# Turning H of groups 3 to 15 by a transposing DMA instead of by TensorE in a hypergraph layer

## The chip, the cores and the metric

The kernel runs on one core of one Trainium2 chip. The metric is the device time of one execution in microseconds (us); lower is better. Each instruction stream (TensorE, VectorE, ScalarE, GpSimd and SyncE, in the profile PE, DVE, ACT, POOL and SP) works through its own queue in order and waits on semaphores that the others raise. PEld is TensorE's weight load, which runs beside its matmuls. SP does no arithmetic here; it only issues DMAs.

## The reference

64 graphs of 128 nodes with 256 features each. `adj` is a 128x128 matrix of each graph, about one entry in eight of which is not zero.

```python
H   = (adj != 0)                       # [n, c, e]
w   = adj[:, 0, :]                     # first row of adj: the weight of each hyperedge
Dn  = 1 / sum_e H * w                  # 0 where the sum is not positive
Be  = 1 / sum_c H                      # members of each hyperedge; 0 where none
conv(x, W, b) = Dn * (H @ (Be * (H^T @ (x @ W^T)))) + b

h = layer_norm(relu(conv(x, W1, b1))) * gamma + beta       # 512 wide
y = conv(h, W2, b2) + x                                    # 256 wide
out = layernorm(x + y)
```

## The kernel before

**Tiling.** Four graphs make a group (`PER = 4`), sixteen groups the run (`G = 16`). Everything of a group lies as 128 partitions x 4 graphs x columns. The two convolutions of a graph share one matrix, A = Dn H Be H^T, which is made once in 128x128 and then applied to x (before W1) and to the second layer's product (after W2).

**How A is made.** VectorE compares `adj_sb` with zero and writes `h_sb` in bf16 (`make_h`, L533). TensorE turns the four 128x128 blocks into the PSUM bank `bank_h` (`turn_h`, L201 to L207). ScalarE copies them to `ht_sb` in f32, block by block, and sums each row on the way, which counts the members of each hyperedge (`read_ht`, L393 to L401: per block one ACTIVATE and one read of the accumulator). VectorE inverts the counts (`make_b`), ScalarE scales (`make_htb`, L408), TensorE multiplies (`make_s`, L217), ScalarE scales by Dn (`make_a`, L416), TensorE turns the result (`turn_a`), and ScalarE stores it as `at_sb` (`read_at`, L424). H is prepared three groups ahead of its use in the second half of a group, and `h_sb`, `ht_sb` have two buffers each.

**The two layers.** `make_u` (L238) is A x; `make_v` (L253) is u W1^T, four chunks k = 0 to 3 of six matmuls each, since u and W1 are split into a high and a low part; `relu` (L436) and `square` (L443) on ScalarE take a chunk each from the two halves of `bank_v` in turn; GpSimd and VectorE split r into `r_hi` (L789) and `r_lo` (L595); `make_g` (L261, L263, L268) is r W2^T, one graph at a time; `read_g` (L586) applies the first normalisation, `make_y` (L285) applies A in two halves of two graphs, `make_z` (L615) adds the residual and `normalise` (L448) finishes.

**What sets the order.** All five streams are written out by hand, one iteration per group, with semaphores between them; there is no scheduler. TensorE's iteration i is: g(i,0), u(i+1), s(i+2), g(i,1), v(i+1,0), g(i,2), turn_q(i), turn_a(i+2), g(i,3), v(i+1,1), turn_h(i+3), v(i+1,2), v(i+1,3), y(i,0), y(i,1). The piece of ScalarE's iteration beside the end of it is relu(i+1,1), read_ht(i+3), relu(i+1,2), square(i+1,1), relu(i+1,3), square(i+1,2), square(i+1,3), make_htb(i+3). `make_y(i, 1)` needs the half of `bank_v` that relu(i+1,3) reads, so it waits for it. SyncE's iteration is the load of adj(i+6), the load of x(i+3), which waits for GpSimd's `add_b2` (L781), and the store of group i-1. Turns of H stand in TensorE's queue for groups 0 to 2 in the preamble and iteration 0, and for groups 3 to 15 in iterations 0 to 12; iteration 13 and later have none.

Of the kernel before, what the change touches and what calls it, by code (L numbers as in the profile page):

```python
# [6 lines left out]
ACT = mybir.ActivationFunctionType  # L7
F32 = mybir.dt.float32
F32R = mybir.dt.float32r
BF16 = mybir.dt.bfloat16  # L10

P = 128
PER = 4
# [6 lines left out]
def hypergraph_block(nc, x, adj, W1, b1, gamma, beta, W2, b2, out):  # L20
# [4 lines left out]
    G = N // PER  # L25
# [8 lines left out]
    with ExitStack() as ctx:  # L34
        def sb(name, shape, dt=F32):
            return ctx.enter_context(nc.sbuf_tensor(name, shape, dt))

        def sem(name):
            return ctx.enter_context(nc.semaphore(name))
# [28 lines left out]
        x_sb = sb("x_sb", [P, 3, PER, DIN])  # L68
        xb_sb = sb("xb_sb", [P, 2, PER, DIN])
        h_sb = sb("h_sb", [P, 2, PER, P], BF16)  # L70
        ht_sb = sb("ht_sb", [P, 2, PER, P])
        members = sb("members", [P, PER])
        binv = sb("binv", [P, 2, PER])
# [31 lines left out]
        bank_h_bf = bank_h.bitcast(BF16)  # L105
        s_parts = bank_s[:, :, 0:2 * HCOLS].rearrange("p b (n e) -> p b n e", n=2)
        last_z = [bank[:, 0:DOUT] for bank in (bank_v[:, 0], bank_v[:, 1], bank_h, bank_q)]
        SUM = DOUT

        weights_in = [sem(f"weights_in{n}") for n in range(4)]  # L110
        edges_in, edges_turned, edges_ready = sem("edges_in"), sem("edges_turned"), sem("edges_ready")
# [8 lines left out]
        w2_hi_ready, w2_ready = sem("w2_hi_ready"), sem("w2_ready")  # L120
        beta_ready, c2_made, c2_ready = sem("beta_ready"), sem("c2_made"), sem("c2_ready")
        h_ready, h_turned, ht_ready = sem("h_ready"), sem("h_turned"), sem("ht_ready")
        b_step, b_ready, htb_ready, wcol_ready = sem("b_step"), sem("b_ready"), sem("htb_ready"), sem("wcol_ready")
        s_made, degree_step, d_ready = sem("s_made"), sem("degree_step"), sem("d_ready")
        a_ready, a_turned, at_ready = sem("a_ready"), sem("a_turned"), sem("at_ready")
# [10 lines left out]
        def graph(n):  # L136
            return slice(n * P, (n + 1) * P)

        def graphs(half):
            return slice(0, PER) if half is None else slice(half * (PER // 2), (half + 1) * (PER // 2))  # L140

        def each(half):
            return range(PER)[graphs(half)]

        def landed(j, ring):

            return 16 * (j // ring + 1)
# [5 lines left out]
        @block.sync  # L153
        def _(sp):
            def load_adj(j):
                if j >= 3:
                    sp.wait_ge(h_ready, j - 2)
                sp.dma_start(adj_sb[:, j % 3], adj_dram[:, j * PER:(j + 1) * PER]).then_inc(adj_in[j % 3], 16)

            def load_x(j):  # L160
                if j >= 3:
                    sp.wait_ge(u_made, (j - 2) * KD)
                    sp.wait_ge(xb_ready, j - 2)
                sp.dma_start(x_sb[:, j % 3], x_dram[:, j * PER:(j + 1) * PER]).then_inc(x_in[j % 3], 16)

            def store(i, half=None):
                part, n = graphs(half), len(each(half))
                if half is None:
                    sp.wait_ge(out_ready, i + 1)
                else:  # L170
                    sp.wait_ge(last_out_ready, half + 1)
                sp.dma_start(out_dram[:, i * PER + part.start:i * PER + part.start + n],
                             z_sb[:, i % 2, part]).then_inc(stored[i % 2], 16)

            load_adj(0)
            sp.dma_start(w1_raw[:, :, :], W1.rearrange("(k p) d -> p k d", p=P)).then_inc(weights_in[1], 16)
            sp.dma_start(w2_raw[:, :, :], W2.rearrange("(k p) h -> p k h", p=P)).then_inc(weights_in[2], 16)
            load_x(0)
            load_adj(1)
            load_adj(2)  # L180
            load_x(1)
            sp.dma_start(b2_half[:, :], b2.unsqueeze(0).to_broadcast([P, DOUT])).then_inc(weights_in[3], 16)
            load_adj(3)
            load_x(2)
            load_adj(4)
            load_adj(5)
            for i in range(G):
                if i + 6 < G:
                    load_adj(i + 6)
                if i + 3 < G:  # L190
                    load_x(i + 3)
                if i >= 1:
                    store(i - 1)
            for half in range(2):
                store(LAST, half)
            sp.wait_ge(stored[0], 16 * (G // 2))
            sp.wait_ge(stored[1], 16 * (G // 2) + 16)

        @block.tensor
        def _(pe):  # L200
            def turn_h(j):  # L201
                pe.wait_ge(h_ready, j + 1)
                if j:
                    pe.wait_ge(at_ready, j)
                for n in range(PER):
                    mm = pe.transpose(bank_h_bf[:, graph(n)], h_sb[:, j % 2, n], ident_b[:, :])
                mm.then_inc(h_turned, 1)  # L207
# [49 lines left out]
            def make_g(i, n):  # L257
                for k in range(KH):
                    if n == 0:
                        pe.wait_ge(r_hi_ready, i * KH + (k + 1))  # L260
                    pe.matmul(bank_g[:, n, 0:W2COLS], r_hi[:, i % 2, k, graph(n)], w2_hi[:, k],  # L261
                              start=(k == 0), stop=False)
                    pe.matmul(bank_g[:, n, 0:DOUT], r_hi[:, i % 2, k, graph(n)], w2_lo[:, k], start=False, stop=False,  # L263
                              skip_group_check=True)
                for k in range(KH):
                    if n == 0:
                        pe.wait_ge(r_lo_ready, i * KH + (k + 1))
                    mm = pe.matmul(bank_g[:, n, 0:W2COLS], r_lo[:, i % 2, k, graph(n)], w2_hi[:, k], start=False,  # L268
                                   stop=(k == KH - 1))
                if n == PER - 1 or (i == LAST and n == PER // 2 - 1):  # L270
                    mm.then_inc(g_made, 1)

            def turn_q(i):
                pe.wait_ge(q_ready, i + 1)
                pe.wait_ge(q_summed, i)
                pe.wait_ge(a_ready, min(i + 3, G))
                for n in range(PER):
                    mm = pe.transpose(bank_q[:, graph(n)], q_sb[:, graph(n)], ident[:, :])
                mm.then_inc(q_turned, 1)
# [61 lines left out]
            for i in range(G):  # L341
                last = i == LAST
                make_g(i, 0)
                if i == 0:
                    turn_h(2)
                if not last:
                    make_u(i + 1)
                if 0 < i and i + 2 < G:
                    make_s(i + 2)
                if i == 0:  # L350
                    pe.wait_ge(c2_ready, 1)
                make_g(i, 1)
                if i == 0:
                    make_s(2)
                if last:
                    turn_q(i)
                else:
                    make_v(i + 1, 0)
                make_g(i, 2)
                if not last:  # L360
                    turn_q(i)
                if i + 2 < G:
                    turn_a(i + 2)
                make_g(i, 3)
                if last:
                    break
                make_v(i + 1, 1)
                if i + 3 < G:
                    turn_h(i + 3)
                make_v(i + 1, 2)  # L370
                make_v(i + 1, 3)
                make_y(i, 0)
                make_y(i, 1)
# [17 lines left out]
        @block.scalar  # L391
        def _(act):
            def read_ht(j):  # L393
                act.wait_ge(h_turned, j + 1)
                act.wait_ge(b_ready, j)
                if j >= 2:
                    act.wait_ge(s_made, j - 1)
                for n in range(PER):
                    ins = nc.scalar.activation(ht_sb[:, j % 2, n], bank_h_bf[:, graph(n)], ACT.Copy,
                                               accum_out=members[:, n:n + 1])  # L400
                ins.then_inc(ht_ready, 1)  # L401

# [125 lines left out]
        def _(dve):  # L528
            def make_h(j):
                dve.wait_ge(adj_in[j % 3], landed(j, 3))  # L530
                if j >= 2:
                    dve.wait_ge(h_turned, j - 1)
                nc.vector.tensor_scalar(h_sb[:, j % 2], adj_sb[:, j % 3], 0.0, None,  # L533
                                        ALU.not_equal).then_inc(h_ready, 1)

# [25 lines left out]
            def make_var1(i, half=None):  # L561
                part, done = graphs(half), i + (half or 0)
                dve.wait_ge(g_made, done + 1)
                nc.vector.tensor_scalar(stat1[:, 0, part], bank_g[:, part, SUM], 1.0 / HID, None,  # L564
                                        ALU.mult).then_inc(stat1_step, 1)
# [189 lines left out]
            for half in range(2):  # L755
                dve.wait_ge(rstd2_ready, G + half)
                for n in each(half):
                    ins = nc.vector.tensor_scalar(z_sb[:, 1, n], last_z[n], mean2[:, 1, n:n + 1],
                                                  rstd2[:, 1, n:n + 1], ALU.add, ALU.mult)
# [112 lines left out]
```

## Time and profile before

| | us |
|---|---|
| median of 3 runs | 301.17 (300.36 to 301.25) |
| the profiled execution | 300.86 |
| its span, first to last instruction | 299.1 |
| TensorE busy | 285.9 (96%) |
| VectorE, ScalarE, GpSimd busy | 207.1, 207.4, 133.7 |
| mean granted TensorE clock | 0.988 of full speed |

The table is read so: TensorE's queue is nearly full, the other three are not, and the whole run has fifteen periods of nearly equal length with a start of some 24 us before them and a tail of some 10 us behind them. Busy time is what the hardware records of instructions; matmuls overlap, so a busy TensorE need not be one that does all it could.

### The profile page before, as it was taken

To read this page: it belongs to the slowest core of one execution; us is meant where nothing else is said; L and a number is where in the kernel's file an instruction comes from. 1 tells how busy PE (TensorE), PEld (TensorE's weight loads), DVE (VectorE), ACT (ScalarE), POOL (GpSimd) and SP (SyncE) were. 2 spreads that over 40 slices of the span, in tenths; PEclk is the share of its full clock that TensorE was granted. 3 is DMA by queue.
4 is the path that set the end of the run, shared out by engine and by line. 5 is a ranking of instruction groups with operands and counts; after the bars stand their busy time and mean duration, and the time that the engine had idled before them with its cause. 6 is when DMAs were issued, how large, how long until landed. Compare 5 with 4: busy or idle time off the path is not lost.

```text
span 299.1 us, 5864 instructions
## 1 busy us (share of the span) xinstructions
PE 285.9 (96%) x1918; PEld 254.5 (85%) x1918; DVE 207.1 (69%) x589; ACT 207.4 (69%) x619; POOL 133.7 (45%) x162
## 2 busy tenths in 40 slices
PE   5799999999999999999999999999999999999972
PEld 5689889798988989898898979898897989988851
DVE  1783686794939587593958669494958759394965
ACT  3498577868687786868677786858778686756430
POOL 2233444617353552636344361735355263636441
PEclk9999999999999999999999999999999999999995
DMA  7921030503114050502305050310304040101112
GB/s 217 297 72 36 1 107 0 175 2 125 56 30 148 0 179 0 172 7 57 120 1 175 2 176 2 109 34 8 133 3 140 2 141 0 59 13 37 37 50 90
DMA packets 26437, 22.55 MB, mean 75 GB/s; under 512 B 860, under 2 KB 26152, under 8 KB 26408
## 3 DMA queue, kind: packets, MB, share of 16 engines
q1 hardware_dynamic: 26304, 22.15, 23.5%
q8 instruction: 15, 0.25, 0.3%
q14 instruction: 14, 0.11, 0.1%
q10 hardware_dynamic: 104, 0.04, 0.0%
HBM read 13.80 MB, written 8.39 MB: 74 GB/s over the span
## 4 chain that ended last, share of the span: by engine, by line
DVE 32%; POOL 27%; issue 23%; PE 11%; ACT 3%; DMA 2%; DVEq 0%; POOLq 0%; SPq 0%
POOL xb_sb L781 11%; DVE r_lo L595 7%; POOL rstd L774 7%; DVE g_sb L586 6%; DVE bn_sb L623 6%; DVE z_sb L615 6%; POOL rstd L796 5%; PE bank_v L253 4%; POOL r_hi L789 4%; DVE mv_sb L633 2%; DMA w_raw<-in_L_gnn_W_dram 2%; PE bank_v L238 1%; POOL shift L801 1%; DVE mean L636 1%; DVE u_lo L558 1%
## 5 line engine op out<-in xcount | busy, mean ns | idle before, releaser
L789 POOL TENSOR_SCALAR r_hi<-r_sb 128x512 fp32r<-128x512 f32 x64 | 48.2, 753 | 82.4 <-ACT r_sb L436 82.4
L261 PE MATMUL bank_g<-w_hi,r_hi 128*128 128x258 f32 x256 | 69.3, 303 | 0.0
L263 PE MATMUL bank_g<-w_lo,r_hi 128*128 128x256 f32 x256 | 63.8, 281 | 0.0
L436 ACT ACTIVATE r_sb<-bank_v,vec 128x512 f32<-128x512 f32 x64 | 44.2, 690 | 15.8 <-PE bank_v L253 15.8
L253 PE MATMUL bank_v<-u_hi,w_hi 128*128 128x512 f32 x128 | 51.9, 406 | 0.4 <-DVE u_lo L558 0.4
L253 PE MATMUL bank_v<-u_lo,w_hi 128*128 128x512 f32 x128 | 50.5, 395 | 0.0
L253 PE MATMUL bank_v<-u_hi,w_lo 128*128 128x512 f32 x128 | 50.4, 394 | 0.0
L263 PEld LDWEIGHTS bank_g<-w_lo,r_hi 128*128 128x128 f32 x256 | 48.4, 189 | 1.0
L261 PEld LDWEIGHTS bank_g<-w_hi,r_hi 128*128 128x128 f32 x256 | 48.3, 189 | 1.1
L595 DVE TENSOR_TENSOR r_lo<-r_sb,r_hi 128x512 fp32r<-128x512 f32 x64 | 47.6, 747 | 1.5 <-POOL r_hi L789 1.5
L268 PE MATMUL bank_g<-w_hi,r_lo 128*128 128x258 f32 x256 | 41.3, 283 | 0.0
L796 POOL TENSOR_TENSOR rstd<-var,half_power 128x4 f32<-128x4 f32 (+1 forms) x17 | 16.7, 980 | 51.3 <-DVE var L637 51.3
L781 POOL TENSOR_TENSOR xb_sb<-x_sb,b_half 128x1024 f32<-128x1024 f32 x16 | 38.2, 2385 | 2.7 <-DVE q_sb L606 2.7
L443 ACT ACTIVATE sq_sb<-r_sb 128x512 f32<-128x512 f32 x64 | 38.3, 625 | 0.5
L586 DVE SCALAR_TENSOR_TENSOR g_sb<-bank_g,rstd,c 128x256 f32<-128x256 f32 x64 | 26.6, 477 | 17.1 <-POOL rstd L774 17.1
L430 ACT ACTIVATE u_hi<-bank_v 128x512 fp32r<-128x512 f32 x32 | 19.0, 598 | 26.5 <-PE bank_v L238 26.5
L564 DVE TENSOR_SCALAR stat<-bank_g 128x4 f32<-128x4 f32 (+1 forms) x17 | 2.7, 161 | 50.1 <-PE bank_g L268 50.1
L448 ACT ACTIVATE z_sb<-z_sb,shift,rstd 128x256 f32<-128x256 f32 x60 | 33.0, 614 | 3.2 <-POOL shift L801 3.2
L268 PEld LDWEIGHTS bank_g<-w_hi,r_lo 128*128 128x128 f32 x256 | 35.2, 189 | 0.0
L285 PE MATMUL bank_v<-g_sb,at_sb 128*128 128x256 f32 x120 | 31.9, 388 | 0.1
L238 PE MATMUL bank_v<-at_sb,x_sb 128*128 128x128 f32 x256 | 31.3, 275 | 0.7 <-ACT at_sb L424 0.7
L238 PEld LDWEIGHTS bank_v<-at_sb,x_sb 128*128 128x128 f32 x256 | 30.0, 192 | 0.9 <-ACT at_sb L424 0.9
(95 smaller groups left out, 485.2 us busy)
## 6 DMA issues: line engine op xcount, KB each, us to landing
x_sb<-in_x_dram SPq DMA_DIRECT2D x16, 512.0 KB, 3.8
out_dram<-z_sb SPq DMA_DIRECT2D x15, 512.0 KB, 4.6
adj_sb<-in_adj_dram SPq DMA_DIRECT2D x16, 256.0 KB, 5.0
w_raw<-in_L_gnn_W_dram SPq DMA_DIRECT2D x2, 512.0 KB, 6.2
out_dram<-z_sb SPq DMA_DIRECT2D x2, 256.0 KB, 2.2
b_half<-in_L_gnn_b_dram SPq DMA_DIRECT2D x1, 128.0 KB, 7.3
edge_rows<-in_adj_dram ACTq DMA_DIRECT2D x1, 32.0 KB, 3.2
vec_rows<-in_L_gnn_b_dram ACTq DMA_DIRECT2D x1, 2.0 KB
```

The source lines that it names most:

```text
L238: mm = pe.matmul(bank_v[:, c, graph(n)], x_sb[:, j % 3, n, graph(c)], at_sb[:, j % 3, n], start=True, stop=True)
L253: mm = pe.matmul(bank_v[:, k % 2], w[:, c, graph(k)], u[:, c], start=(m == 0), stop=(m == len(terms) - 1))
L261: pe.matmul(bank_g[:, n, 0:W2COLS], r_hi[:, i % 2, k, graph(n)], w2_hi[:, k], start=(k == 0), stop=False)
L263: pe.matmul(bank_g[:, n, 0:DOUT], r_hi[:, i % 2, k, graph(n)], w2_lo[:, k], start=False, stop=False, skip_group_check=True)
L268: mm = pe.matmul(bank_g[:, n, 0:W2COLS], r_lo[:, i % 2, k, graph(n)], w2_hi[:, k], start=False, stop=(k == KH - 1))
L436: nc.scalar.activation(r_sb[:, k], bank_v[:, k % 2], ACT.Relu, bias=vec[:, k:k + 1]).then_inc(relu_ready, 1)
L443: nc.scalar.activation(sq_sb[:, k], r_sb[:, k], ACT.Square).then_inc(sq_ready, 1)
L448: ins = nc.scalar.activation(z_sb[:, i % 2, n], z_sb[:, i % 2, n], ACT.Identity, bias=shift2[:, n:n + 1], scale=rstd2[:, 0, n:n + 1])
L586: ins = nc.vector.scalar_tensor_tensor(out=g_sb[:, n], in0=bank_g[:, n, 0:DOUT], scalar=rstd1[:, n:n + 1], in1=c2[:, :], op0=ALU.mult, op1 ...
L595: nc.vector.tensor_tensor(r_lo[:, i % 2, k], r_sb[:, k], r_hi[:, i % 2, k].bitcast(F32), ALU.subtract).then_inc(r_lo_ready, 1)
L781: nc.gpsimd.tensor_tensor(xb_sb[:, i % 2], x_sb[:, i % 3], b2_half[:, :].unsqueeze(1).to_broadcast([P, PER, DOUT]), ALU.add).then_inc(xb_r ...
L789: nc.gpsimd.tensor_scalar(r_hi[:, i % 2, k], r_sb[:, k], 1.0, 1.0, ALU.mult, ALU.mult).then_inc(r_hi_ready, 1)
```

## The change

H of groups 3 to 15 goes through a new buffer in SBUF, `turned_h`, which has the shape and the type of `h_sb` and two buffers. SyncE issues one transposing DMA per group, which reads the four blocks of `h_sb` and writes their transposes side by side. It waits for the comparison of its group, for the transposing DMA before it, and, from group 5 on, for ScalarE's reading of the buffer that it overwrites. `read_ht` takes its blocks from `turned_h` instead of PSUM, and `make_h` waits for the DMA where it waited for TensorE's turn. TensorE keeps the turns of groups 0 to 2.

```diff
@@ sync @@
+            def turn_h(j):
+                sp.wait_ge(h_ready, j + 1)
+                if j > ON_PE:
+                    sp.wait_ge(h_dma_turned, 16 * (j - ON_PE))
+                if j >= ON_PE + 2:
+                    sp.wait_ge(ht_ready, j - 1)
+                sp.dma_start_transpose(turned_h[:, j % 2], h_sb[:, j % 2].rearrange("p n c -> p (n c)")).then_inc(
+                    h_dma_turned, 16)
...
             load_adj(5)
+            turn_h(3)
             for i in range(G):
                 if i + 6 < G:
                     load_adj(i + 6)
+                if i + 4 < G:
+                    turn_h(i + 4)
                 if i + 3 < G:
                     load_x(i + 3)
@@ tensor @@
                 make_v(i + 1, 1)
-                if i + 3 < G:
-                    turn_h(i + 3)
                 make_v(i + 1, 2)
@@ scalar, read_ht @@
-                act.wait_ge(h_turned, j + 1)
+                if j < ON_PE:
+                    act.wait_ge(h_turned, j + 1)
+                else:
+                    act.wait_ge(h_dma_turned, 16 * (j - ON_PE + 1))
...
-                    ins = nc.scalar.activation(ht_sb[:, j % 2, n], bank_h_bf[:, graph(n)], ACT.Copy,
+                    source = bank_h_bf[:, graph(n)] if j < ON_PE else turned_h[:, j % 2, n]
+                    ins = nc.scalar.activation(ht_sb[:, j % 2, n], source, ACT.Copy,
@@ vector, make_h @@
-                if j >= 2:
+                if 2 <= j < ON_PE + 2:
                     dve.wait_ge(h_turned, j - 1)
+                elif j >= ON_PE + 2:
+                    dve.wait_ge(h_dma_turned, 16 * (j - 2 - ON_PE + 1))
```

TensorE's queue in iteration 0, where v(1,1) ends and v(1,2) begins (`bank_v` is written from the split u and W1; L253 before is L268 of the changed kernel). Before:

```order
109 L253 MATMUL bank_v<-u_hi,w_hi 128x512
110 L253 MATMUL bank_v<-u_hi,w_lo 128x512
111 L253 MATMUL bank_v<-u_lo,w_hi 128x512
112 L206 MATMUL bank_s<-ident_b,h_sb 128x128 [waits at_ready,h_ready]
113 L206 MATMUL bank_s<-ident_b,h_sb 128x128 x3
114 L253 MATMUL bank_v<-u_hi,w_hi 128x512 [waits relu_ready]
115 L253 MATMUL bank_v<-u_hi,w_lo 128x512
```

and in the changed kernel:

```order
109 L268 MATMUL bank_v<-u_hi,w_hi 128x512
110 L268 MATMUL bank_v<-u_hi,w_lo 128x512
111 L268 MATMUL bank_v<-u_lo,w_hi 128x512
112 L268 MATMUL bank_v<-u_hi,w_hi 128x512 [waits relu_ready]
113 L268 MATMUL bank_v<-u_hi,w_lo 128x512
```

The four turning matmuls are gone and the next chunk of v follows at once; the other rows keep their order. SyncE's queue in iterations 1 and 2, one load of adj, one of x and one store each. Before:

```order
12 L158 DMA adj_sb<-in_adj_dram 128x4x128 [waits h_ready]
13 L164 DMA x_sb<-in_x_dram 128x4x256 [waits xb_ready,u_made]
14 L172 DMA out_dram<-z_sb 128x4x256 [waits out_ready]
15 L158 DMA adj_sb<-in_adj_dram 128x4x128 [waits h_ready]
16 L164 DMA x_sb<-in_x_dram 128x4x256 [waits xb_ready,u_made]
17 L172 DMA out_dram<-z_sb 128x4x256 [waits out_ready]
```

and in the changed kernel:

```order
15 L161 DMA adj_sb<-in_adj_dram 128x4x128 [waits h_ready]
16 L175 DMA_TRANSPOSE turned_h<-h_sb 128x4x128 [waits ht_ready,h_dma_turned,h_ready]
17 L167 DMA x_sb<-in_x_dram 128x4x256 [waits xb_ready,u_made]
18 L184 DMA out_dram<-z_sb 128x4x256 [waits out_ready]
19 L161 DMA adj_sb<-in_adj_dram 128x4x128 [waits h_ready]
20 L175 DMA_TRANSPOSE turned_h<-h_sb 128x4x128 [waits ht_ready,h_dma_turned,h_ready]
21 L167 DMA x_sb<-in_x_dram 128x4x256 [waits xb_ready,u_made]
22 L184 DMA out_dram<-z_sb 128x4x256 [waits out_ready]
```

The transposing DMA stands between the load of adj and the load of x, so both that load and the store behind it are queued behind its three waits.

## Rows read from the trace of the kernel before

**Rows 1.** The page: busy time, share of the span and instructions of each engine
```profile
PE 285.9 (96%) x1918; PEld 254.5 (85%) x1918; DVE 207.1 (69%) x589; ACT 207.4 (69%) x619; POOL 133.7 (45%) x162
```

**Rows 2.** Timeline of PE: start us, duration us, engine, line, operation, out<-in, count
```profile
139.76 0.39 PE L253 MATMUL bank_v<-u_lo,w_hi 128*128 128x512 f32 x1
139.99 0.40 PE L206 MATMUL bank_s<-ident_b,h_sb 128*128 128x128 bf16 x4
140.19 0.48 PE L253 MATMUL bank_v<-u_hi,w_hi 128*128 128x512 f32 x1
140.51 0.39 PE L253 MATMUL bank_v<-u_hi,w_lo 128*128 128x512 f32 x1
```

**Rows 3.** Timeline of PE: the y matmuls of iterations 11, 12 and 13
```profile
228.77 2.13 PE L285 MATMUL bank_v<-g_sb,at_sb 128*128 128x256 f32 x8
...
245.91 2.13 PE L285 MATMUL bank_v<-g_sb,at_sb 128*128 128x256 f32 x8
...
262.77 0.38 PE L285 MATMUL bank_v<-g_sb,at_sb 128*128 128x256 f32 x1
```

**Rows 4.** Timeline of PE: y of one iteration, its fourth and fifth record alone
```profile
143.08 2.13 PE L285 MATMUL bank_v<-g_sb,at_sb 128*128 128x256 f32 x8
143.72 0.38 PE L285 MATMUL bank_v<-g_sb,at_sb 128*128 128x256 f32 x1
144.11 0.45 PE L285 MATMUL bank_v<-g_sb,at_sb 128*128 128x256 f32 x1
```

**Rows 5.** Timeline of ACT beside it; in brackets idle time before, and its releaser
```profile
140.18 0.69 ACT L436 ACTIVATE r_sb<-bank_v,vec 128x512 f32<-128x512 f32 x1 [0.66 <-PE bank_v L253]
140.77 0.27 ACT L399 ACTIVATE ht_sb<-bank_s 128x128 f32<-128x128 bf16 x1
...
141.02 0.28 ACT L399 ACTIVATE ht_sb<-bank_s 128x128 f32<-128x128 bf16 x1
...
141.87 0.69 ACT L436 ACTIVATE r_sb<-bank_v,vec 128x512 f32<-128x512 f32 x1
142.46 0.62 ACT L443 ACTIVATE sq_sb<-r_sb 128x512 f32<-128x512 f32 x1
143.28 0.69 ACT L436 ACTIVATE r_sb<-bank_v,vec 128x512 f32<-128x512 f32 x1 [0.19 <-PE bank_v L253]
143.86 1.14 ACT L443 ACTIVATE sq_sb<-r_sb 128x512 f32<-128x512 f32 x2
```

**Rows 6.** Groups of ACT, 100 to 240 us: busy us, mean ns of one, idle before
```profile
L408 ACT ACTIVATE htb_sb<-ht_sb,binv 128x128 f32<-128x128 f32 x32 | 10.2, 393 | 0.0
L416 ACT ACTIVATE a_sb<-bank_s,dinv 128x128 f32<-128x128 f32 x33 | 9.5, 368 | 9.9 <-DVE dinv L545 9.9
```

**Rows 7.** Timelines of DVE and of PEld behind read_g of the same iteration
```profile
141.22 1.66 DVE L586 SCALAR_TENSOR_TENSOR g_sb<-bank_g,rstd,c 128x256 f32<-128x256 f32 x4 [0.99 <-POOL rstd L774]
...
145.20 0.69 DVE L595 TENSOR_TENSOR r_lo<-r_sb,r_hi 128x512 fp32r<-128x512 f32 x1
...
146.25 0.19 PEld L268 LDWEIGHTS bank_g<-w_hi,r_lo 128*128 128x128 f32 x1
```

**Rows 8.** Timelines of DVE (the comparison) and of SP's DMA issues
```profile
139.55 0.38 SPq L172 DMA_DIRECT2D out_dram<-z_sb  x1
...
152.12 0.42 DVE L533 TENSOR_SCALAR h_sb<-adj_sb 128x512 bf16<-128x512 f32 x1
...
156.13 0.37 SPq L164 DMA_DIRECT2D x_sb<-in_x_dram  x1
```

**Rows 9.** Timelines of DVE and ACT at the start: comparison and reading of group 3
```profile
25.11 0.42 DVE L533 TENSOR_SCALAR h_sb<-adj_sb 128x512 bf16<-128x512 f32 x1
...
37.91 0.27 ACT L399 ACTIVATE ht_sb<-bank_s 128x128 f32<-128x128 bf16 x1
```

**Rows 10.** The page: a DMA queue (packets, MB, share of 16 engines) and issues (KB, us to landing)
```profile
q1 hardware_dynamic: 26304, 22.15, 23.5%
...
out_dram<-z_sb SPq DMA_DIRECT2D x15, 512.0 KB, 4.6
```

More of the change, by code:

```diff
@@ L70, in hypergraph_block @@
         h_sb = sb("h_sb", [P, 2, PER, P], BF16)
+        turned_h = sb("turned_h", [P, 2, PER, P], BF16)
         ht_sb = sb("ht_sb", [P, 2, PER, P])
@@ L108, in hypergraph_block @@
         SUM = DOUT
+        ON_PE = 3
         weights_in = [sem(f"weights_in{n}") for n in range(4)]
@@ L122, in hypergraph_block @@
         h_ready, h_turned, ht_ready = sem("h_ready"), sem("h_turned"), sem("ht_ready")
+        h_dma_turned = sem("h_dma_turned")
         b_step, b_ready, htb_ready, wcol_ready = sem("b_step"), sem("b_ready"), sem("htb_ready"), sem("wcol_ready")
```

## The prediction

> **What bounds the kernel now.** The page's busy line comes first: TensorE is busy for 96% of the span and no other engine for more than 69% [rows 1]. The next view is TensorE's timeline, to see whether "busy" is a queue that never waits. From one y to the next the iterations repeat at 245.91 - 228.77 = 17.14 us [rows 3], and inside one the matmuls follow at a fixed step; only at y does one come late. The first four records of y step by (143.72 - 143.08) / 3 = 0.21 us, so the fifth was due at 143.93 and starts at 144.11, 0.18 us late [rows 4]. It begins the second half of y, which waits for ScalarE's fourth relu: that starts at 143.28, lasts 0.69 and ends at 143.97 [rows 5]. So a period is TensorE's own work with one short stall, and a change is worth what it takes out of TensorE's queue, as long as the chains on ScalarE and VectorE beside it can move up by as much. That is the question here; the profiled execution took 300.86 us, 0.31 below the median of 301.17, and the sum is made on the first and carried over to the second.
>
> **What is removed from TensorE.** In an iteration the four turning matmuls start at 139.99, 0.23 after the last matmul of v(i+1,1) at 139.76, which is that chunk's own step. The first two matmuls of v(i+1,2) start at 140.19 and 140.51 [rows 2]. Without the turns these two would start at 139.99 and 140.22, so the four cost 140.51 - 140.22 = 0.29 us; the start at 140.19 shows nothing, because the next step behind it is 0.32 instead of 0.23. The trace holds a control for this number: iteration 13 has no turn. Its y starts at 262.77, 16.86 us after that of iteration 12, against 17.14 before [rows 3]. The difference is 0.28 us, and in iteration 13 TensorE did take it. There are 13 such iterations (0 to 12), which makes 13 x 0.28 = 3.6 us if nothing else holds.
>
> The Trainium skill, "VectorE: DVE Perf Modes", section "The three transpose paths", gives 390 ns for a 128x128 bf16 transpose on TensorE, which for four would be an estimated 1.56 us per group and 20 us in all. The trace disagrees: four in a row take 0.28 us out of the queue.
>
> **What iteration 13 does not test: ScalarE.** It has no read_ht either, and the change keeps read_ht, with another source. The chain is relu(k=1) at 140.18, read_ht from 140.77, relu(k=2) at 141.87, square at 142.46, relu(k=3) at 143.28 [rows 5]. The blocks of read_ht step by 141.02 - 140.77 = 0.25, so four of them leave ScalarE free at 141.77; relu(k=2) waited 0.10 more for TensorE. Reading SBUF instead of PSUM costs more: no row shows this copy from SBUF in bf16, but the two scaled 128x128 copies differ by their source, 393 ns from SBUF and 368 from PSUM [rows 6], 0.025 more. The lower bound is then nothing (a two-byte source may be no dearer), the upper one twice the row's difference, 0.05 per block, since the step can grow by more than the duration; the row's value, 0.03, is taken. With 4 x 0.03 = 0.12 relu(k=2) starts at 141.89, square at 142.48. A relu behind a square can start 0.52 after it (two squares last 1.14 together and one alone 0.62 [rows 5]), so at 143.00. TensorE's v(i+1,3) would be done for a start at 143.28 - 0.28 = 143.00. The fourth relu moves up by the whole 0.28; by the upper bound, relu(k=3) starts at 143.08 and moves up by 0.20. The 0.18 stall of y stays, since both sides move together.
>
> **VectorE behind it.** Its queue from read_g at 141.22 is anchored to the end of g(i,3), which lies ahead of the removed turns, and runs without a gap to r_lo(k=3), at 145.20 for 0.69, done 145.89. TensorE loads that as a weight in g(i+1,0) at 146.25 [rows 7], and 0.28 earlier at 145.97. The margin falls from 0.36 to 0.08. What a handover costs is bounded by nothing below and, from the nearest row, by the 0.14 between the end of the relu at 143.97 and the y matmul at 144.11 [rows 4, 5]; with that one the weight is ready at 146.03, and 0.06 of the gain is lost. Between 0.22 and 0.28 I take 0.26, because on both chains the middle value still fits. Each shorter period ends at the next g(i+1,3), from which VectorE's queue starts anew, so the loss does not add up. The sum: 13 x 0.26 = 3.4 us; 300.86 - 3.4 = 297.5 for an execution like the profiled one, 301.17 - 3.4 = **297.8** as median. The ends are 13 x 0.20 = 2.6 and 13 x 0.29 = 3.8.
>
> **What is added: 13 transposing DMAs.** No row shows one. In steady state the comparison that feeds it ends at 152.12 + 0.42 = 152.54 [rows 8]. By ScalarE's row this H is read one iteration later than its turn would now be possible: read_ht of the iteration shown is at 140.77 [rows 5], that of the next at 157.9, and the H made at 152.12 belongs to the one after that, at 140.77 + 34.3 = 175.1. The cover is 22.5 us. For group 3, at the start, it is from 25.53 to 37.91, 12.4 us [rows 9]. The price from below is the nearest ordinary transfer, a store of 512 KB that lands 4.6 us after its issue [rows 10]; this one has 128 KB. The price from above follows from pieces: the queue's 26,304 packets took 23.5% of 16 engines' time over the span of 299.1 us, 42.8 ns each [rows 10]; 65,536 pieces of one element each would take 65,536 x 42.8 ns / 16 = 175 us. I take about 5 us, since rows of 256 bytes and more, 512 pieces, come to 1.4 us by the same rate and the landing dominates. Then all of it is covered.
>
> The Trainium skill speaks against the change here: "VectorE: DVE Perf Modes", section "Rules for kernel authors", advises TensorE for a 128x128 transpose whenever PSUM will do as destination, and the table of "The three transpose paths" gives 1309 ns per block on the DMA path. Four would be an estimated 5.2 us, inside the cover, so the sum would be the same by it.
>
> **What it moves on queues.** SyncE's queue gains one issue per iteration, and its wait ends at 152.54, while the load of x behind it goes at 156.13 anyway for another reason [rows 8]. If SyncE is held for less than 3.6 us per transpose, neither the load nor the store behind it moves at all; an ordinary issue holds it for 0.37 to 0.38. If it is held longer, the store (139.55 + 17.15 = 156.70 in that period) slides, and what it must beat is VectorE's writing of the same z buffer a group later, just ahead of r_lo(k=3) two periods on from 145.20, so about 178.9. With 4.6 to land there are over 17 us left. VectorE's comparison waits for a transpose of two groups earlier, done 20 us before. ScalarE's `read_ht` gets the only new wait that matters: behind it are relu(k=2), the squares and relu(k=3), and TensorE's v, y and g wait for those.
>
> **Rivals.**
> 1. *The gain is taken up by ScalarE or VectorE.* If a read from `turned_h` steps by 0.055 to 0.08 more (the fourth relu moves up by 0.40 less four times that), or GpSimd and VectorE slow each other in the new alignment, a period shrinks by 0.07 to 0.18: 1 to 2.3 us, 298.9 to 300.3. For it: three chains are within 0.1 us of each other. Against: iteration 13 took the full 0.28 with two of them in place.
> 2. *Nothing is gained, since the read grows by 0.10 per block.* relu(k=2) then starts at 142.17, 0.30 later than now, relu(k=3) at 143.28 again, and the time is 301 within 0.9. For it: no row of this form. Against: the SBUF reads of rows 6 are 0.025 apart from the PSUM ones.
> 3. *Slower: the transposing DMA is the new bound.* If the DMA works in pieces so small that it takes longer than a period, the loop runs at the DMA's time T, because each transpose waits for the one before, ScalarE waits in read_ht, and everything waits for ScalarE: 301.2 + 13 x (T - 17.15). It decides from T = 17.15 us, which is 6,400 pieces of 42.8 ns on 16 engines, or 20 bytes a piece; at T = 20 the time is 338, and at one piece per element (175 us) 2,350. For it: a transpose in two-byte elements has no long rows on both sides. Against: nothing in the trace. The same sign comes at a small size if T is between 12.4 and 17: only the first turn is late, by under 5 us, once, which the gain nearly repays.
> 4. *The change does not do what it says*, in that TensorE stays as long although its turns are gone. Iteration 13 excludes it but for rival 2.
>
> **How the numbers follow.** My forecast, the whole or nearly the whole of 0.20 to 0.29 per iteration, has 0.62: 13 x that gives 297.4 to 298.6, with the spread of the runs (0.4) 297.0 to 299.0. Rival 1 has 0.13, rivals 2 and 4 together 0.11, rival 3 and other slowdowns by over 0.9 us 0.10; 0.04 is left for below 297.0. The measurement can tell about 0.3%, 0.9 us, from no change. So faster is 0.62 + 0.13 + 0.04 = 0.79, within 0.3% 0.11, slower 0.10. For eight in ten the range takes the forecast, rival 1 and the near part of rival 2: 296.9 to 300.7.
>
> **What would show it.** Right: the y matmuls 16.86 to 16.9 us apart in iterations 1 to 12 and unchanged in 13; no turning matmul beyond the first three groups; ScalarE's blocks of read_ht 0.25 to 0.30 apart with no idle time before the first; the load of x still released by GpSimd. Wrong by rival 1: a later fourth relu or a weight load of r_lo that waits. Wrong by rival 3: ScalarE idle before read_ht with a DMA as releaser, SyncE waiting for transposes, and the store late. The forecast fails if the transposing DMA holds SyncE or the DMA engines for a large part of a period, or if its traffic slows engines that read SBUF, for which no row gives a price.

## The result, and the profile after

The changed kernel takes 299.65 us (median of 20 runs, 299.42 to 301.02) against 301.12 (median of 20 runs of the kernel before beside it). The ratio is 0.9965, 95% interval 0.9954 to 0.9976: faster, by about 1.05 us. (The medians lie 1.47 us apart. Executions of either kernel scatter over more than 1 us; the means of the 20 differ by 1.07, and the ratio follows these.) One execution of e8_split_g_wait took 1,585 us and is left out of its ratio. The forecast was faster by 3.4 us, to 297.8. The sign was right and the time lies in the range, but the gain is under a third of the one forecast.

The page of the changed kernel, its busy line, its DMA queue and the issues of the new kind (no KB are given for it; the last number is the median us from issue to landing):

```profile
PE 284.8 (96%) x1866; PEld 253.0 (85%) x1866; DVE 209.9 (70%) x589; ACT 206.8 (69%) x619; POOL 132.9 (45%) x162
...
q1 hardware_dynamic: 33376, 23.86, 27.1%
...
turned_h<-h_sb SPq DMA_TRANSPOSE x13, 2.4
```

TensorE has lost its 52 turning matmuls (x1918 to x1866, [rows 1]) but its busy time fell by only 1.1 us, and VectorE, of which nothing was removed or added, is busy for 2.8 us more. The transposing DMAs land after 2.4 us, at most 3.6, far inside the cover of 12 and 22 us.

The timeline of TensorE gives the period by its y matmuls, as [rows 3] do for the kernel before:

```profile
39.76 2.17 PE L300 MATMUL bank_v<-g_sb,at_sb 128*128 128x256 f32 x8
...
56.84 2.17 PE L300 MATMUL bank_v<-g_sb,at_sb 128*128 128x256 f32 x8
...
261.91 2.13 PE L300 MATMUL bank_v<-g_sb,at_sb 128*128 128x256 f32 x8
...
277.42 2.13 PE L300 MATMUL bank_v<-g_sb,at_sb 128*128 128x256 f32 x8
```

A period is 17.08 to 17.10 us, where 16.86 to 16.9 was forecast and 17.14 was before. The y of iteration 14, the last of this form, stands at 277.42 against 278.28 before, 0.86 us earlier. The first y brings 0.46 of that (39.76 against 40.22). It has the removed turn of iteration 0 ahead of it, worth 0.28; the rest belongs to the start, which varies from one execution to the next: in e1_dma_beside below, with the same queue on TensorE as before, the first y stands at 41.12. The twelve intervals up to iteration 12 bring 0.63, 0.05 each instead of 0.28. And the interval to iteration 13, which was 16.86 before, is 17.09 now and gives 0.23 back. The profiled executions themselves differ by more, 300.86 and 299.62; the other 0.4 us lies in the tail. From the y at 278.28 to the end of the span there are 20.8 us before and 20.3 after, and the granted clock of the last slice was 0.5 before and 0.8 after. The change isn't the reason: e1_dma_beside and e5_order_on_before keep every turn on TensorE, and from their y of iteration 14 to the end there are 20.3 and 20.5 us.

So something new ends late in each period. First VectorE's queue and GpSimd in the kernel before, two instructions of each (r_lo and r_hi are one line for every chunk; r_lo(k) and r_hi(k) are those of chunk k, in order):

```profile
142.79 1.01 DVE L595 TENSOR_TENSOR r_lo<-r_sb,r_hi 128x512 fp32r<-128x512 f32 x1
...
144.01 0.68 DVE L595 TENSOR_TENSOR r_lo<-r_sb,r_hi 128x512 fp32r<-128x512 f32 x1
...
142.64 0.62 POOL L789 TENSOR_SCALAR r_hi<-r_sb 128x512 fp32r<-128x512 f32 x1 [0.94 <-ACT r_sb L436]
144.04 1.12 POOL L789 TENSOR_SCALAR r_hi<-r_sb 128x512 fp32r<-128x512 f32 x1 [0.78 <-ACT r_sb L436]
```

VectorE's queue behind read_g in the changed kernel, the place of [rows 7]:

```profile
140.77 1.66 DVE L605 SCALAR_TENSOR_TENSOR g_sb<-bank_g,rstd,c 128x256 f32<-128x256 f32 x4 [0.99 <-POOL rstd L793]
142.35 1.01 DVE L614 TENSOR_TENSOR r_lo<-r_sb,r_hi 128x512 fp32r<-128x512 f32 x1
...
143.57 0.89 DVE L614 TENSOR_TENSOR r_lo<-r_sb,r_hi 128x512 fp32r<-128x512 f32 x1
144.38 0.68 DVE L634 SCALAR_TENSOR_TENSOR z_sb<-xb_sb,bank_v 128x512 f32<-128x512 f32 x1
144.98 0.68 DVE L614 TENSOR_TENSOR r_lo<-r_sb,r_hi 128x512 fp32r<-128x512 f32 x1
```

GpSimd beside it, r_hi of k = 2 and 3 and the small copy behind them:

```profile
142.20 0.62 POOL L808 TENSOR_SCALAR r_hi<-r_sb 128x512 fp32r<-128x512 f32 x1 [0.94 <-ACT r_sb L453]
143.29 0.62 POOL L808 TENSOR_SCALAR r_hi<-r_sb 128x512 fp32r<-128x512 f32 x1 [0.47 <-ACT r_sb L453]
143.87 0.64 POOL L787 COPY htb_sb<-edge_cols 128x4 f32<-128x4 f32 x1
```

And TensorE's matmuls and its weight loads at the end of g(i+1,0) and the start of u:

```profile
142.29 2.17 PE L300 MATMUL bank_v<-g_sb,at_sb 128*128 128x256 f32 x8
145.26 0.83 PE L283 MATMUL bank_g<-w_hi,r_lo 128*128 128x258 f32 x4
145.93 1.95 PE L253 MATMUL bank_v<-at_sb,x_sb 128*128 128x128 f32 x16
...
145.14 0.75 PEld L283 LDWEIGHTS bank_g<-w_hi,r_lo 128*128 128x128 f32 x4
```

r_lo(2) takes 0.89 us. In the kernel before, the same instruction took 0.68 at 144.01, and GpSimd's r_hi(3), 0.03 behind it at 144.04, took 1.12. Now r_hi(3) starts at 143.29, 0.28 ahead of r_lo(2), and takes 0.62: which of the two starts first has changed, because the fourth relu, and with it r_hi(3), moved up with TensorE, while VectorE's queue did not. r_lo(3) is done at 144.98 + 0.68 = 145.66. The four weight loads of r_lo, 0.12 apart, would have the last at 145.50; four in 0.75 us, each 0.19 long, put it at 145.70. TensorE waits 0.19 us there in every period, and the next matmuls (u) start 0.67 after the first of r_lo, where it was 0.49 before.

That closes the account of a period. The turns take 0.29 out of it (from the first matmul of v(i+1,1) to y: 4.48 us before, 4.19 after), the wait for r_lo(3) puts 0.19 back, and ScalarE puts 0.04 back: its fourth relu moved up by 0.25 and not by 0.29 (it stands 2.85 behind the second one, 3.10 before), so the second half of y starts 1.07 behind the first instead of 1.03. What is left is 0.06, and the periods show 0.05.

A second, smaller delay of the same kind lies ahead of it. VectorE's statistics after g(i,3) contain one product of two 128x4 tiles in SBUF:

```profile
155.59 0.21 DVE L586 TENSOR_TENSOR stat<-stat 128x4 f32<-128x4 f32 x1
...
153.40 2.38 POOL L800 TENSOR_TENSOR xb_sb<-x_sb,b_half 128x1024 f32<-128x1024 f32 x1
```

It starts while GpSimd's add (153.40 to 155.78) still runs and takes 0.21; before, the add ended at 138.92, the product started at 139.00 and took 0.16. Together VectorE's chain is about 0.26 us longer than the forecast had it.

The Trainium skill, "SBUF — State Buffer", section "SBUF: two separate sides", says that VectorE and GpSimd share one pair of SBUF ports, and that where VectorE has two inputs in SBUF and GpSimd reads SBUF, the one that starts first keeps the pair for its whole instruction while the other stands still. No trace shows the ports, but the times agree: r_hi(3) ends at 143.91 and r_lo(2) 0.55 behind it, at 144.46, though it started 0.34 before that end; r_lo(1) of the kernel before ends 0.54 behind r_hi(2) (143.80 and 143.26). The other way round, r_hi(3) of the kernel before ends 0.47 behind r_lo(2) (145.16 and 144.69). In these rows the one that starts second ends some half a microsecond behind the end of the first, however long it has waited.

### The profile page after: what moved, and what is told of

Same layout as the page of the kernel before. It is cut to its first block, busy times and chain, and to the rows that moved or that the text cites. A ratio compares the mean times of both kernels' runs of the same rounds, so it can differ in the third digit from the quotient of the medians.

```text
span 297.7 us, 5772 instructions
## 1 busy us (share of the span) xinstructions
PE 284.8 (96%) x1866; PEld 253.0 (85%) x1866; DVE 209.9 (70%) x589; ACT 206.8 (69%) x619; POOL 132.9 (45%) x162
## 3 DMA queue, kind: packets, MB, share of 16 engines
q1 hardware_dynamic: 33376, 23.86, 27.1%
## 4 chain that ended last, share of the span: by engine, by line
DVE 34%; POOL 28%; issue 25%; PE 8%; ACT 3%; DVEq 0%; POOLq 0%
POOL xb_sb L800 11%; DVE r_lo L614 8%; POOL rstd L793 7%; DVE bn_sb L642 7%; DVE z_sb L634 6%; DVE g_sb L605 6%; POOL rstd L815 5%; POOL r_hi L808 4%; PE bank_v L268 3%; DVE mv_sb L652 2%; PE bank_s L333 1%; POOL shift L820 1%; DVE mean L655 1%; DVE u_lo L577 1%; ACT ht_sb L416 1%
## 5 line engine op out<-in xcount | busy, mean ns | idle before, releaser
L808 POOL TENSOR_SCALAR r_hi<-r_sb 128x512 fp32r<-128x512 f32 x64 | 41.8, 654 | 78.0 <-ACT r_sb L453 78.0
L614 DVE TENSOR_TENSOR r_lo<-r_sb,r_hi 128x512 fp32r<-128x512 f32 x64 | 50.3, 790 | 1.5 <-POOL r_hi L808 1.5
L268 PE MATMUL bank_v<-u_hi,w_hi 128*128 128x512 f32 x128 | 50.9, 397 | 0.4 <-DVE u_lo L577 0.4
L268 PE MATMUL bank_v<-u_lo,w_hi 128*128 128x512 f32 x128 | 50.6, 395 | 0.0
L268 PE MATMUL bank_v<-u_hi,w_lo 128*128 128x512 f32 x128 | 50.5, 394 | 0.0
L283 PE MATMUL bank_g<-w_hi,r_lo 128*128 128x258 f32 x256 | 43.8, 288 | 0.0
L283 PEld LDWEIGHTS bank_g<-w_hi,r_lo 128*128 128x128 f32 x256 | 36.1, 189 | 1.7
L253 PE MATMUL bank_v<-at_sb,x_sb 128*128 128x128 f32 x256 | 31.3, 275 | 0.7 <-ACT at_sb L441 0.7
L433 ACT ACTIVATE a_sb<-bank_s,dinv 128x128 f32<-128x128 f32 x60 | 17.2, 369 | 21.0 <-DVE dinv L564 21.0
```

The lines of the kernel that those rows point to most:

```text
L268: mm = pe.matmul(bank_v[:, k % 2], w[:, c, graph(k)], u[:, c], start=(m == 0), stop=(m == len(terms) - 1))
L614: nc.vector.tensor_tensor(r_lo[:, i % 2, k], r_sb[:, k], r_hi[:, i % 2, k].bitcast(F32), ALU.subtract).then_inc(r_lo_ready, 1)
L808: nc.gpsimd.tensor_scalar(r_hi[:, i % 2, k], r_sb[:, k], 1.0, 1.0, ALU.mult, ALU.mult).then_inc(r_hi_ready, 1)
```

## The experiments

The theory: the gain was lost to this collision. The rivals: the transposing DMAs or their hold on SyncE cost it (traffic), or ScalarE's dearer reads from SBUF do. The fences show the main lines of each edit.

### e1_dma_beside: the transposing DMAs alone, beside the old kernel

```diff
             load_adj(5)
+            turn_h(3)
...
                     load_adj(i + 6)
+                if i + 4 < G:
+                    turn_h(i + 4)
```

`make_h` also waits for the transposing DMA of two groups earlier, as in the changed kernel.

> The kernel before, with the 13 transposing DMAs added at the places of the change and nobody reading what they write; TensorE keeps all its turns and ScalarE reads PSUM. Collision theory (the gain was lost because GpSimd's r_hi(3) now runs first and holds up VectorE's r_lo(2)): the DMAs cost nothing, 301.1 us, ratio 1.000 within 0.001, y matmuls 17.14 us apart. Traffic rival (the transposing DMAs or their hold on SyncE cost the 2.2 us that are missing): about 303.3 us, ratio 1.007.

Measured: 301.35 us, ratio 1.0008 (0.9996 to 1.0021), periods of 17.12 to 17.16. The DMAs cost nothing that can be told from noise, at most 0.6 us by the interval, where over 2 us are missing. Traffic falls.

### e2_no_dma: the change without the DMAs

```diff
-                    source = bank_h_bf[:, graph(n)] if j < ON_PE else turned_h[:, j % 2, n]
+                    source = bank_h_bf[:, graph(n)] if j < ON_PE else h_sb[:, j % 2, n]
```

The thirteen DMAs are gone from SyncE, ScalarE waits for the comparison instead, and `make_h` for ScalarE's reading.

> The changed kernel without any transposing DMA: ScalarE reads the untransposed h_sb for groups 3 to 15, so H is not turned there and this part of the computation is left out. Same reads from SBUF, same instructions on all engines but SyncE. Collision theory: as the changed kernel, 299.6 us, ratio 0.995 to 0.997, y 17.08 apart, r_lo(2) 0.89 us long. Traffic rival: the missing gain appears, 297.5 us, ratio 0.988.

Measured: 299.61 us, ratio 0.9962 (0.9946 to 0.9978), periods of 17.07 to 17.09. r_lo(2) and r_hi(3) stand as in the changed kernel:

```profile
143.46 0.89 DVE L602 TENSOR_TENSOR r_lo<-r_sb,r_hi 128x512 fp32r<-128x512 f32 x1
...
143.18 0.62 POOL L796 TENSOR_SCALAR r_hi<-r_sb 128x512 fp32r<-128x512 f32 x1 [0.47 <-ACT r_sb L441]
```

Whatever holds the gain back is there without a single transposing DMA.

### e3_order: another order of VectorE's queue

```diff
-                split_r(i + 1, 1)
                 if i + 3 < G:
                     make_b(i + 3)
-                split_r(i + 1, 2)
+                split_r(i + 1, 1)
                 if i + 1 < LAST:
                     make_z(i, 0)
+                    split_r(i + 1, 2)
                     split_r(i + 1, 3)
```

> The changed kernel with VectorE's queue behind read_g in the order b, r_lo(1), z(i,0), r_lo(2), r_lo(3), z(i,1) instead of r_lo(1), b, r_lo(2), z(i,0), r_lo(3), z(i,1): the same instructions, but r_lo(1) and r_lo(2) no longer start while GpSimd works on an r_hi. Collision theory: both take 0.69 us, r_lo(3) ends about 0.3 us earlier, TensorE no longer waits for it, y 16.86 to 16.91 apart, 297.6 to 298.2 us, ratio 0.988 to 0.991. Traffic rival, and the rival that ScalarE's slower reads from SBUF bind: 299.6, ratio 0.996.

Measured: 297.92 us, ratio 0.9895 (0.9877 to 0.9912). Its periods are 16.88 to 16.90. VectorE and GpSimd:

```profile
141.28 0.49 DVE L569 TENSOR_SCALAR binv<-members 128x4 f32<-128x4 f32 x1
...
141.90 0.68 DVE L614 TENSOR_TENSOR r_lo<-r_sb,r_hi 128x512 fp32r<-128x512 f32 x1
142.50 0.68 DVE L634 SCALAR_TENSOR_TENSOR z_sb<-xb_sb,bank_v 128x512 f32<-128x512 f32 x1
143.09 1.29 DVE L614 TENSOR_TENSOR r_lo<-r_sb,r_hi 128x512 fp32r<-128x512 f32 x2
...
142.22 0.83 POOL L809 TENSOR_SCALAR r_hi<-r_sb 128x512 fp32r<-128x512 f32 x1 [0.47 <-ACT r_sb L453]
```

r_lo(1) takes 0.68 and the last two 1.29 together. The same instructions, with the same reads from SBUF and the same DMAs, are 1.7 us faster than in the changed kernel by the medians, 2.1 by the ratios. With the reads from SBUF and the DMAs unchanged, neither rival can have held that part back, and 3.2 of the 3.4 us forecast are there. (The first small operation of b takes 0.49 here instead of 0.16, while GpSimd's r_hi(2) runs until 141.75; so some of the blocked time is only moved to where it costs less. It has one input in SBUF, so it isn't only instructions with two that are held.)

### e4_pool_waits: the old order, with GpSimd made to start second

```diff
                 split_r(i + 1, 2)
+                if i + 3 < G:
+                    pool.wait_ge(b_ready, i + 4)
                 split_r(i + 1, 3)
```

> The changed kernel with one more wait: GpSimd starts r_hi(3) only when VectorE's b of the same iteration is done, so that VectorE's r_lo(2) starts first again, as in the kernel before. Collision theory: r_lo(2) takes 0.69 us again instead of 0.89, r_hi(3) grows from 0.62 to about 1.1, y 16.86 to 16.95 apart, 297.8 to 298.6 us, ratio 0.989 to 0.992. Rivals that put the loss elsewhere (traffic, ScalarE's reads): 299.6 or a little more, ratio 0.996.

Measured: 297.81 us, ratio 0.9891 (0.9874 to 0.9908), periods of 16.87 to 16.89. One added wait on the engine that has time:

```profile
142.48 0.68 DVE L614 TENSOR_TENSOR r_lo<-r_sb,r_hi 128x512 fp32r<-128x512 f32 x1
...
143.67 0.69 DVE L614 TENSOR_TENSOR r_lo<-r_sb,r_hi 128x512 fp32r<-128x512 f32 x1
...
142.65 0.99 POOL L808 TENSOR_SCALAR r_hi<-r_sb 128x512 fp32r<-128x512 f32 x1 [0.91 <-DVE binv L572]
...
144.06 0.55 PEld L283 LDWEIGHTS bank_g<-w_hi,r_lo 128*128 128x128 f32 x4
```

r_lo(2) is back to 0.68, r_hi(3) pays with 0.99, r_lo(3) ends at 144.36, and the four weight loads take 0.55, as in a queue that doesn't wait: the last starts at 144.42, 0.06 behind r_lo(3), where the forecast had left a margin of 0.08. No more than this just fits. With r_lo(2) at its old length, which the prediction had taken for granted, the time is the one predicted. Delaying one engine made the whole faster, and only a collision between the two explains that. No kernel here was measured faster than this one and e3_order.

### e5_order_on_before: the other order on the kernel before

The diff is that of e3_order, on the kernel before.

> The kernel before (TensorE turns all H, no transposing DMA) with VectorE's queue in the order b, r_lo(1), z(i,0), r_lo(2), r_lo(3), z(i,1), the order that together with the change gave 0.9895. Collision theory: without the removed turns TensorE's own queue is the bound, r_lo(3) had 0.36 us of margin already, so nothing is gained: 301.1 us, ratio 1.000 within 0.001, y 17.14 apart. Rival (the order by itself is what gained 1.7 us there): 299.4, ratio 0.994.

Measured: 301.27 us, ratio 1.0006 (0.9993 to 1.0019), periods of 17.13 to 17.16. The order by itself gains nothing: there TensorE's queue was the bound. What e3_order gained is the change's, given back.

### e6_read_turned: the read from SBUF alone

```diff
-                act.wait_ge(h_turned, j + 1)
+                if j < 3:
+                    act.wait_ge(h_turned, j + 1)
+                else:
+                    act.wait_ge(h_dma_turned, 16 * (j - 2))
...
+                    source = bank_h_bf[:, graph(n)] if j < 3 else turned_h[:, j % 2, n]
```

> The kernel before with the transposing DMAs added and ScalarE reading their result from SBUF, while TensorE still makes its (now unused) turns. It tells what the read from SBUF costs by itself. My term: the blocks of read_ht step by 0.28 to 0.29 instead of 0.25, relu(2) starts about 0.08 later against relu(1), relu(3) still waits for TensorE: 301.2 us, ratio 1.000 within 0.001. Rival (ScalarE's reads take part of the gain): slower than before by 13 times 0.1 or more, 302.5, ratio 1.004.

Measured: 302.02 us, ratio 1.0047 (1.0028 to 1.0067). My expectation missed, and the rival's number (1.004) is the one that came; but the trace shows another mechanism than the rival's. The periods are of two kinds: 17.13 to 17.15 in six of the twelve up to iteration 12, and 17.33 or 17.34 in the six others. Two periods, VectorE's r_lo(2) and GpSimd's r_hi(3) of each, the first followed by an interval of 17.14 and the second by one of 17.34:

```profile
58.36 0.68 DVE L615 TENSOR_TENSOR r_lo<-r_sb,r_hi 128x512 fp32r<-128x512 f32 x1
...
58.34 1.17 POOL L809 TENSOR_SCALAR r_hi<-r_sb 128x512 fp32r<-128x512 f32 x1 [0.73 <-ACT r_sb L454]
...
92.83 1.14 DVE L615 TENSOR_TENSOR r_lo<-r_sb,r_hi 128x512 fp32r<-128x512 f32 x1
...
92.81 0.62 POOL L809 TENSOR_SCALAR r_hi<-r_sb 128x512 fp32r<-128x512 f32 x1 [0.72 <-ACT r_sb L454]
```

In both the two start within 0.02 us of each other. Where VectorE wins, GpSimd takes 1.17 and the period is that of the kernel before; where GpSimd wins, r_lo(2) takes 1.14 and the period is 0.2 longer. This holds for all twelve: r_lo(2) takes 1.13 or 1.14 in exactly the six long ones. e1_dma_beside, with the same DMAs but the old reads, has none. ScalarE's reads (blocks 0.29 apart) start relu(2) and r_hi(2) a few hundredths later, r_lo(1) ends later behind r_hi(2) (1.05 long instead of 1.01), and that brings r_lo(2) level with r_hi(3). Six times 0.19 is 1.1 of the 1.4 us. So the reads do cost time here, but through the collision: the fourth relu itself stands 3.09 us behind the second one, as before (3.10). ScalarE's reads are not harmless in every alignment.

### e7_split_g and e8_split_g_wait: filling the stall of y as well

```diff
                 make_y(i, 0)
+                make_g(i + 1, 0, 0)
                 make_y(i, 1)
```

on e3_order (e7_split_g) and on e4_pool_waits (e8_split_g_wait). The added call issues the matmuls of k = 0 and 1 of r_hi, which g(i+1,0) then leaves out.

> e3_order with the first four matmuls of g(i+1,0) (k = 0 and 1 of r_hi) moved between y(i,0) and y(i,1) on TensorE, to fill the time in which y(i,1) waits for the fourth relu, 0.18 to 0.25 us per iteration over 15 iterations. If that stall is real time of TensorE and nothing else is next within 0.25 us: 297.9 - 3.0 = 294.5 to 295.5, ratio 0.978 to 0.982, y(i,1) no longer late. If VectorE's chain from the end of g(i,3) to r_lo(3) or GpSimd is the bound by now: 297 to 298, ratio 0.987 to 0.990.

> The same move of four matmuls of g(i+1,0), on e4_pool_waits. There VectorE's chain to r_lo(3) is 0.58 us longer than in e3_order (the old order, with r_lo(1) taking 1.01), so by the collision theory r_lo(3) should bind again and part of the gain of the move be lost: 296.5 to 297.8, ratio 0.985 to 0.989, and TensorE late at the last weight of g(i+1,0). If r_lo(3) plays no part: the same as e7_split_g, 294.5 to 295.5.

Measured: 298.13 us, ratio 0.9902 (0.9883 to 0.9921), and 297.94 us, ratio 0.9895 (0.9875 to 0.9914). Neither gains on its parent; the periods are 16.87 to 16.90 in both. In the first, TensorE's waits in its iterations (who waits, for whom: us, times, longest) show that the weight loads of y wait 13 times instead of 27, for 2.9 us instead of 7.9. The wait before the second half of y is gone, the one before the first half is left, and there is a new one:

```profile
PEld bank_v L302 <- issue: 2.9, 13, 0.2
PEld bank_g L285 <- DVE r_lo L617: 2.2, 13, 0.2
```

So its second alternative held: VectorE's chain to r_lo(3) is the bound once TensorE would be faster by another 0.2 us. (The median of 298.13 is just outside the 297 to 298 given for it.) For the second, I expected 296.5 to 297.8 with r_lo(3) as the bound; the median of 297.94 is just outside too. The list of waits has none of TensorE for r_lo, but it leaves out waits under 0.15 us, and the timeline shows two short ones. The matmuls of r_hi(3) come 0.09 late, since r_hi(3) ends at 144.57, and the four matmuls of r_lo take 0.77 instead of the 0.65 of a queue that doesn't wait, since r_lo(3) ends at 145.29 and the fourth weight load was due at 145.21:

```profile
143.58 0.99 POOL L811 TENSOR_SCALAR r_hi<-r_sb 128x512 fp32r<-128x512 f32 x1 [0.91 <-DVE binv L575]
...
144.60 0.69 DVE L617 TENSOR_TENSOR r_lo<-r_sb,r_hi 128x512 fp32r<-128x512 f32 x1
...
144.51 0.28 PE L278 MATMUL bank_g<-w_lo,r_hi 128*128 128x256 f32 x1
144.63 0.38 PE L276 MATMUL bank_g<-w_hi,r_hi 128*128 128x258 f32 x1
144.84 0.28 PE L278 MATMUL bank_g<-w_lo,r_hi 128*128 128x256 f32 x1
144.96 0.77 PE L285 MATMUL bank_g<-w_hi,r_lo 128*128 128x258 f32 x4
```

So r_lo(3) is the last to be ready in both. In e3_order, e4_pool_waits, e7_split_g and e8_split_g_wait alike it ends 3.16 or 3.17 us behind the start of y. The premise of my second expectation, that the old order makes this chain 0.58 longer than e3_order's, was wrong, and a faster TensorE finds no margin in either.

How much went to the two extra switches between y and g on TensorE (the first matmul of g after y is followed after 0.30 instead of 0.12 us) was not separated.

## Why the prediction was right and wrong

**TensorE's queue: right.** Four turns cost 0.28 to 0.29 us per iteration, and with e4_pool_waits a period fell from 17.14 to 16.88, 0.26, the value that the sum used. That the value came out so exactly is in part luck: the sum took it as a middle between two bounds, for a loss at the handover of r_lo(3). In e4_pool_waits nothing is lost there (the four weight loads of r_lo take the 0.55 of a queue that doesn't wait); the second half of y starts 1.06 to 1.07 behind the first instead of 1.03, and that is ScalarE's side.

**The added DMAs: right.** They landed in 2.4 us, where about 5 was taken, held SyncE for 1.19 us as a rule, and cost nothing that shows (e1_dma_beside, 1.0008). Rival 3 is out.

**ScalarE: nearly right within the change.** The blocks step by 0.29 instead of 0.25, a little more than the 0.03 taken. So the fourth relu moved up by 0.25, not by the whole 0.28: relu(3) in the changed kernel starts at 142.54, where ScalarE, not TensorE, is just the later one, and y's stall grows by 0.04. In e4_pool_waits, whose gain is whole but for 0.02 per period, this costs next to nothing. Outside the change, in e6_read_turned, the same reads cost 1.4 us, most of it by shifting the collision, for which the prediction had no step.

**VectorE behind it: wrong, and this is the step that failed.** The prediction said that its queue "runs without a gap to r_lo(k=3), at 145.20 for 0.69", and moved TensorE and ScalarE up against it with every duration in it kept. The order of the queue and its anchor were right. Its durations were not properties of the instructions: they depended on when GpSimd's r_hi starts, and r_hi(3) hangs on the fourth relu, which was the thing that the sum moved by 0.28. What the runs showed in its place: r_lo(2) takes 0.89 instead of 0.68 as soon as r_hi(3) starts ahead of it, and 0.68 again when r_hi(3) is made to wait (e4_pool_waits), with the whole gain. The rows for it stood in the trace of before, r_hi(3) with 1.12 us and r_lo(1) with 1.01 where others of their kinds take 0.62 and 0.69. I read them as slow and did not ask who was making whom wait. The chain grew by 0.26 where 0.08 of margin was left; that took 0.19 of the 0.28 in each of twelve periods (ScalarE took 0.04), and with ScalarE's part 0.23 in the interval to iteration 13, which had no turn to lose.

**The control, iteration 13, was read too widely.** The r_lo(3) that TensorE loads between the y of iteration 12 and that of 13 was made in iteration 12, which still had its turn, so it still had its margin of 0.36. The next one, which met the shorter queue, comes behind the y of iteration 13, and VectorE has no b there: r_lo(2) follows r_lo(1) at once and r_lo(3) is early (1.85 us behind y instead of 2.12). The control tested TensorE's term and no other, and the prediction used it against rival 1 ("took the full 0.28 with two of them in place").

**Rival 1 is what happened.** It named this ("GpSimd and VectorE slow each other in the new alignment") and its 298.9 to 300.3 holds the result; it had a chance of 0.13. The result lies in the stated range because the range took this rival in, not because the sum was right. Its place and price could have been worked out: r_hi(3) 0.28 earlier is ahead of r_lo(2), so GpSimd runs first. By the row of r_lo(1), which ended 0.54 behind the r_hi that had started ahead of it, r_lo(2) then ends at 143.76 + 0.62 + 0.54 = 144.92 instead of 144.69. That is 0.23 later, against a margin of 0.08.

**The handover** that I bounded with 0 to 0.14 us measured about 0.05: r_lo(3) ends at 145.66 and the waiting weight load starts at 145.70 by the rows above, 0.053 apart before rounding.

## What to carry to other kernels

When an edit moves one engine against another, every pair of instructions of VectorE and GpSimd that overlaps must be looked at again: instructions longer than their kind mark the places where one waits for the other, and which of the two it is can flip with a shift of hundredths of a microsecond. Where it flips against the critical engine, the cure is cheap, a wait on the engine with time to spare or another order of independent work on the busy one. A control found inside a trace tests only the terms that are the same in it.

## What the runs showed of the hardware

A transposing DMA of 128x512 bf16 from SBUF to SBUF landed 2.4 us after its issue (median; at most 3.6 in the changed kernel and 4.5 in e4_pool_waits), kept SyncE for 1.19 us (median; at most 2.46) where an ordinary issue in steady state keeps it 0.37 to 0.5, and made (33,376 - 26,304) / 13 = 544 packets. ScalarE's copy of 128x128 bf16 with a row sum stepped by 0.29 us from SBUF and 0.25 from PSUM. r_lo on VectorE, with two SBUF inputs, and r_hi on GpSimd, started within 0.02 us of each other, ran one behind the other, in either order, at 0.68 and 1.17 us or at 1.14 and 0.62. The second ended 0.53 to 0.55 us behind the first where it was VectorE's, and 0.47 to 0.48 where it was GpSimd's, in the kernel before, in the changed kernel, in e4_pool_waits and in e6_read_turned. VectorE's z, with one input in SBUF and one in PSUM, kept its 0.68 in e3_order while r_hi(3) ran beside it.
